# Gated linear attention beside routed experts: differences of the values spread over partitions by a DMA per step instead of by TensorE, and ScalarE as the source of expert weights and biases

## What is computed

```
q = silu(xn Wq) * 16**-0.5;  f = xn Wf;  v = xn Wi;  k = 1 - sigmoid(f)         # 8 heads of 16
S_t = sigmoid(f_t)[:, None] * S_(t-1) + k_t[:, None] * v_t[None, :]             # per head, over 256 tokens
o_t = q_t S_t;   attention = rmsnorm(o) * g_weight @ Wo
# experts: each token goes to 2 of 8, chosen by a hyperbolic distance of project(xn Wp + bp)
# to the centroids, with softmax weights w
experts = sum over the 2 chosen of  w_e * (gelu(xn W1_e + b1_e) W2_e + b2_e)    # 128 -> 512 -> 128
```

## Time and profile before

| | |
|---|---|
| Median of 3 runs | 232.7 us (232.62 to 233.45) |
| Profiled execution, its time | 233.13 us |
| Its span, first to last instruction | 231.4 us |
| Mean granted TensorE clock | 0.911 of full |
| Busy: PE, DVE, POOL, ACT | 191.2, 170.8, 117.6, 104.2 us |
| DMA | 24.45 MB, 106 GB/s |

### The profile page before, as it was taken

How to read it: one execution, slowest core, us unless ns; L and a number is a source line. 1 busy time by engine, 2 the same in 40 slices (tenths; PEclk the granted TensorE clock), 3 DMA queues, 4 the chain that set the end, 5 groups by cost and what they waited for, 6 DMA issues and landing times.

```text
span 231.4 us, 4464 instructions
## 1 busy us (share of the span) xinstructions
PE 191.2 (83%) x1266; PEld 152.0 (66%) x1266; DVE 170.8 (74%) x382; ACT 104.2 (45%) x350; POOL 117.6 (51%) x135
## 2 busy tenths in 40 slices
PE   8692999979589895987999999997789799265890
PEld 7591765456378784867887879886666788123390
DVE  2976930875996986459669979855977687999675
ACT  3439694851364634436434469762554545000011
POOL 7870000002775888776858558787868463302000
PEclk9769799997959998899999999999999999855799
DMA  6681323232753544342334434432444300192015
GB/s 184 178 244 40 97 71 69 46 69 50 221 141 80 130 131 124 82 121 84 118 86 111 122 104 125 146 108 91 125 135 125 81 26 14 29 285 55 0 34 147
DMA packets 21783, 24.45 MB, mean 106 GB/s; under 512 B 2890, under 2 KB 13823, under 8 KB 21760
## 3 DMA queue, kind: packets, MB, share of 16 engines
q1 hardware_dynamic: 17904, 18.91, 29.2%
q0 software_dynamic: 2496, 4.66, 7.6%
q10 hardware_dynamic: 1360, 0.59, 0.9%
HBM read 18.38 MB, written 4.65 MB: 100 GB/s over the span
## 4 chain that ended last, share of the span: by engine, by line
PE 63%; DVE 10%; ACT 10%; issue 8%; another core or an unknown queue 4%; DMA 1%; ACTq 1%; DVEq 0%
PE banks L986 16%; PE banks L976 13%; PE banks L930 6%; PE banks L919 5%; PE banks L837 4%; DVE state L1298 3%; PE banks L968 2%; PE banks L917 2%; ACT xn_t L716 2%; PE banks L835 2%; ACT xn L635 2%; PE banks L954 2%; DVE x_sb L1372 2%; PE banks L792 2%
## 5 line engine op out<-in xcount | busy, mean ns | idle before, releaser
L1298 DVE TENSOR_TENSOR_SCAN state<-gate,banks 128x516 f32<-128x516 f32 x64 | 78.0, 1222 | 21.1 <-PE banks L919 16.4
L475 POOL DMA_INDIRECT xs<-normalised_rows,source x39 | 41.3, 1060 | 49.1 <-DVE source L1283 39.3
L716 ACT ACTIVATE xn_t<-banks,b 128x128 f32<-128x128 f32 x156 | 44.8, 375 | 34.2 <-PE banks L976 25.6
L986 PE MATMUL banks<-w,xn_t 128*128 x312 | 48.6, 287 | 12.2 <-ACT xs_t L709 10.1
L486 POOL DMA_INDIRECT expert_rows_out<-xn_t,place x39 | 42.1, 1081 | 30.5 <-ACT xn_t L725 17.1
L986 PEld LDWEIGHTS banks<-w,xn_t 128*128 128x128 f32 x312 | 41.0, 196 | 20.4 <-issue 20.1
L976 PE MATMUL banks<-xs_t,w 128*128 128x128 f32 x312 | 46.6, 284 | 0.5 <-ACT xs_t L709 0.5
L976 PEld LDWEIGHTS banks<-xs_t,w 128*128 128x128 f32 x312 | 41.5, 199 | 4.0 <-issue 3.4
L919 PE MATMUL banks<-dv,spread 128*128 128x258 f32 x128 | 33.5, 347 | 9.5 <-DVE state L1298 9.5
L1309 DVE TENSOR_TENSOR qstate<-state,q_t 128x512 f32<-128x512 f32 x52 | 36.5, 703 | 0.0
L919 PEld LDWEIGHTS banks<-dv,spread 128*128 128x128 f32 x128 | 20.9, 206 | 14.5 <-DVE state L1298 13.0
(11 more groups left out here) (239 smaller groups left out, 262.1 us busy)
## 6 DMA issues: line engine op xcount, KB each, us to landing
w<-in_L_ffn_W_dram SPq DMA_DIRECT2D x39, 256.0 KB
y_rows<-expert_rows_out SPq DMA_DIRECT2D x8, 256.0 KB, 4.9
x_sb<-_attn_hidden_states_dram SPq DMA_DIRECT2D x4, 256.0 KB, 4.1
normalised_rows<-xn SPq DMA_DIRECT2D x4, 256.0 KB, 2.3
xs<-normalised_rows,source POOLq DMA_INDIRECT x39
expert_rows_out<-xn_t,place POOLq DMA_INDIRECT x39
state<-dv SPq DMA_DIRECT2D x4, 129.0 KB, 2.2
dv<-dv SPq DMA_DIRECT2D x4, 129.0 KB, 2.2
```

The lines of the kernel that those rows point to most:

```text
L475: V.indirect_dma_start(out=xs[t % XRS][:], out_offset=None, in_=xn_dram, in_offset=bass.IndirectOffsetOnAxis(ap=source[:, t:t + 1], axis=0 ...
L716: last = A.activation(hg[t % HGS][:, c * P:(c + 1) * P], bank[6 + t % 2][:, c * P:(c + 1) * P], ACT.Gelu, bias=b1[:, bass.ds(e, 1), c:c + ...
L986: ins = M.matmul(expert_out, hg[t % HGS][:, c * P:(c + 1) * P], w2[:, bass.ds(e, 1), c * D:(c + 1) * D].rearrange("p o f -> p (o f)"), sta ...
L1298: V.tensor_tensor_scan(state[n % STATES][:].rearrange("p b t -> p (b t)"), gate[:, batches_of(g), :].rearrange("p b t -> p (b t)"), pair[n ...
```

## The change

1. **Spread by DMA.** `spread_v`, `less_high_part`, the swaps, `spread`, `minus` and the fp32r tiles are gone. A kind "d" of `project` makes the differences, ACT copies them to `dv_rows[g]` (which are the tiles `state[g]`), SP writes them to DRAM, and for each step SP reads 8 rows of it, each 16 times, into one of `SPREADS = 6` tiles. The scan has both inputs in SBUF. `STATES` is 4, not 6.
2. **Multiplications.** All 64 `times_q` are DVE's.
3. **First weights.** All of W1 (2 MB) is loaded once; ACT copies an expert's part to one of three tiles for each tile of rows.
4. **Biases b2.** All are in SBUF on each partition; ACT writes an expert's row to the PSUM tile in which layer two then accumulates. L917, L1294 and what led to them are gone. `expert_out` is double.
5. **Order of the front.** Centroids and `bp` are turned unnormalised, and what divides by their norm moves behind; ACT squares all 16 routing products (DVE did 6). The counts of the experts stand between `project("d", 2)` and `project("f", 2)`; the values follow the inversion; the "s" projections move into steps 7, 9, 11 and 13. `places()` stands on DVE after the scan of step 2.
6. **Loop and end.** Units are 20 per three steps from step 4 on. Roots of the first three groups are taken together from step 56 on. At the end group 3's expert rows are added around `add_up(3)`, and group 2's last.

```diff
-    STATES = 6
+    STATES = 4
+    SPREADS = 6
-    W1S = 4
+    W1S = 3
-    PER_STEP = 7
-    FIRST_STEP = 2
+    UNITS_OF_STEPS, STEPS_OF_UNITS = 20, 3
+    FIRST_STEP = 4
-    ON_POOL = tuple(n for n in range(5, STEPS) if n % 5 == 0)
+    SUMS_AT = (7, 9, 11, 13)
+    DV_ROW = 576
+    dv_dram = nc.dram_tensor("value_differences", (G, P, DV_ROW), F32).ap()
+        dv = [sb(f"dv{i}", [P, GB, TP]) for i in range(SPREADS)]
+        dv_rows = [state[g][:].rearrange("p b t -> p (b t)") for g in range(G)]
...
# SP
+            def send_differences(g):
+                sp.wait_ge(s_taken, taken("d", g))
+                sp.dma_start(dv_dram[g, :, 0:GB * TP], dv_rows[g]).then_inc(s_dvs[g], 16)
+
+            def load_differences(n):
+                g, j = n // DK, n % DK
+                if n % DK == 0:
+                    sp.wait_ge(s_dvs[g], 16)
+                if n >= SPREADS:
+                    sp.wait_ge(s_scan, n - SPREADS + 1)
+                sp.dma_start(dv[n % SPREADS][:].rearrange("p b t -> p (b t)"),
+                             bass.AP(tensor=dv_dram.tensor, offset=(g * P + first_of(j)) * DV_ROW,
+                                     ap=[[DV_ROW, H], [0, DK], [1, GB * TP]])).then_inc(s_dv[n % SPREADS], 16)
+
+            send_rows(0)
+            send_rows(1)
+            send_differences(0)
+            send_rows(2)
+            send_differences(1)
+            for n in range(SPREADS):
+                load_differences(n)
+            send_rows(3)
+            sp.dma_start(w1[:], w1_in.rearrange("e d f -> d e f")).then_inc(s_w1, 16)
+            sp.dma_start(b2[:], b2_in.unsqueeze(0).to_broadcast([P, E, D])).then_inc(s_b2, 16)
+            send_differences(2)
+            send_differences(3)
+            for n in range(SPREADS, STEPS):
+                load_differences(n)
...
# ACT
+            def first_weights(t, e):
+                if t >= W1S:
+                    act.wait_ge(s_l1, t - W1S + 1)
+                A.copy(w1_of[t % W1S][:], w1[:, bass.ds(e, 1), :].rearrange("p o f -> p (o f)")).then_inc(s_w1of, 1)
+            def bias(t, e):
+                if t >= 2:
+                    act.wait_ge(s_yb, t - 1)
+                A.copy(expert_out[t % 2], b2[:, bass.ds(e, 1), :].rearrange("p o d -> p (o d)")).then_inc(s_b2f, 1)
...
                 if s < TILES:
+                    gelu(s, expert_of(s))
                 if s > 0:
                     expert_rows(s - 1)
+                    if s + 1 < TILES:
+                        bias(s + 1, expert_of(s + 1))
                 if s + 2 < TILES:
                     turned(s + 2)
+                    first_weights(s + 2, expert_of(s + 2))
...
# PE, second layer
+                    pe.wait_ge(s_b2f, t + 1)
+                ins = M.matmul(expert_out[t % 2], hg[t % HGS][:, c * P:(c + 1) * P],
                                w2[:, bass.ds(e, 1), c * D:(c + 1) * D].rearrange("p o f -> p (o f)"),
-                               start=(c == 0), stop=(c == FC - 1))
+                               start=False, stop=(c == FC - 1), skip_group_check=True)
...
# DVE
             def scan(n):
                 g = n // DK
-                dve.wait_ge(s_vb, n + 1)
+                dve.wait_ge(s_dv[n % SPREADS], 16 * (n // SPREADS + 1))
                 dve.wait_ge(s_taken, taken("f", g))
+                if n < G:
+                    dve.wait_ge(s_dvs[n], 16)
...
-                                     pair[n % 2].rearrange("p b t -> p (b t)")[:, BANK - TP:BANK + TP], 0.0,
-                                     ALU.mult, ALU.add).then_inc(s_scan, 1)
+                                     dv[n % SPREADS][:].rearrange("p b t -> p (b t)"), 0.0, ALU.mult, ALU.add).then_inc(s_scan, 1)
...
             scan(0)
             for n in range(STEPS):
                 if n + 1 < STEPS:
                     scan(n + 1)
+                if n == 1:
+                    places()
...
+            g = G - 1
+            dve.wait_ge(s_yg[g], 16 * TOPK)
+            link(add_rows(g, 0))
+            add_up(g)
             dve.wait_ge(s_ot, G)
             V.tensor_tensor(o_sq[:], o_t[:], o_t[:], ALU.mult).then_inc(s_osq, 1)
+            link(add_rows(g, 1))
+            mean(g, added[:, 0:BPG])
```

More of the change, by code:

```diff
@@ L623, in _ @@
             channel_raw(2)
+            for n in range(PER_BANK):
+                squares_of_projection(n)
             channel_raw(3)
[L625 removed]
+            for n in range(PER_BANK, NB):
                 squares_of_projection(n)
[L627 to L631 removed]
             def normalise(g):
@@ L1015, in _ @@
                     pe.wait_ge(s_w2, 16)
-                    pe.wait_ge(s_b2of, BPG)
+                    for rows in expert_out:
+                        last = M.matmul(rows, ident[:], ident[:], start=True, stop=True)
+                    last.then_inc(s_primed, 1)
                     expert_turn(0)
@@ L1327, in finish, with add_attention, roots @@
+            def add_attention(n, rows):
+                return V.scalar_tensor_tensor(out=acc[:, n, :], in0=rows, scalar=rms[:, 1, n:n + 1], in1=x_sb[:, n, :], op0=ALU.mult, op1=ALU.add)
+            def roots(first, last, done):
+                tiles = slice(first * BPG, last * BPG)
+                dve.wait_ge(s_mean, last)
+                for k, ins in enumerate(rsqrt(rms[:, 1, tiles], rms[:, 0, tiles], rms[:, 2, tiles])):
                     ins.then_inc(s_rms, 1)
                     yield
-                    dve.wait_ge(s_rms, done + k + 2)
@@ L1342, in _, with finish_early @@
-            finishing = None
+                    dve.wait_ge(s_rms, done + k + 1)
+            def finish_early():
+                yield from roots(0, EARLY, 0)
+                dve.wait_ge(s_att_sb, EARLY)
+                for g in range(EARLY):
+                    for j in range(BPG):
+                        ins = add_attention(g * BPG + j, att[:, g, j * D:(j + 1) * D])
+                        if j == BPG - 1:
+                            ins.then_inc(s_acc, 1)
+                        yield
@@ L1343, in _, with add_rows @@
+            def add_rows(g, k):
+                for n in range(g * BPG, (g + 1) * BPG):
+                    ins = V.scalar_tensor_tensor(out=acc[:, n, :], in0=y_rows[:, k, n, :], scalar=weight[:, k, n:n + 1],
+                                                 in1=acc[:, n, :], op0=ALU.mult, op1=ALU.add)
+                return ins
+            finishing = finish_early()
             scan(0)
@@ new lines, in _ @@
+                for half in range(2):
+                    if n < DK:
+                        next(of_tokens, None)
+                    elif n >= EARLY * DK + MEAN_AT:
+                        if n == EARLY * DK + MEAN_AT and half == 0:
+                            mean(EARLY - 1, norm2_ps)
+                        else:
+                            for _ in range(FINISH_EACH):
+                                next(finishing, None)
+                    elif n % DK == MEAN_AT and half == 0:
+                        mean(n // DK - 1, norm2_ps)
+                    if half == 0:
+                        times_q(n)
```

622 lines of the change are left out of this document (217 added, 405 removed).

## The result

| | before | after |
|---|---|---|
| Median of 4 runs each | 232.66 us (231.64 to 233.45) | 224.09 us (222.55 to 225.48) |
| Ratio, 95% interval | | 0.963 [0.954, 0.972] |
| Profiled execution, its span | 233.13 us, 231.4 us | 225.48 us, 223.7 us |

Faster, by 3.7%; the prediction was 194 us, 17% faster, with 183 to 213 as its range. The mechanism that it named is there, and 30 us that it counted on are not. Executions of one kernel differ by up to some 5%: a median here is of all of them, a ratio of the faster ones of both kernels.

What follows compares the result with a forecast made beforehand. It saw a ring of PE, DVE and POOL with nearly equal sums as the bound. DVE's 167.6 us, 11.7 for engines holding one another up and 13.3 of end gave a span of 192.6, forecast 194 us, range 183 to 213.

Steps and rivals of the forecast that it cites:

- DVE's own sum: DVE from scan 2 to the last multiplication: 62 x 1.72 us plus 11 us of other work, 117.6 us.
- Front: Ahead of the loop: counts at 31 us, `own` at 40.5, scan 2 waiting for a DMA until 50, first fetch at 52.
- Scan and multiplication: DVE's step in the loop: scan from SBUF kept at 1.22 us, step with multiplication 1.72 us.
- Loads: Differences' loads in the loop: lower half of 0.85 to 2.75 us a step, under DVE's 1.9, hidden by six buffers.
- rival (c): Loads on eight engines at 106 to 157 ns a packet, 2.35 us each, 201 to 205 us; shares chances 0.24 and 0.07.
- the slower rival: DVE waits before the scan for each load, over 2.9 us a load, slower than before; chance 0.07.
- ACT: ACT's work in the loop: 2.54 us a tile, 99 us for 39, some 13 us of other work, 112 us.
- Rival (a): ACT waits 0.5 us per tile, last tile at 182, 205 us in all; shares chance 0.24 for 200 to 213.
- rival (b): POOL's DMAs 0.3 us longer while DVE reads two SBUF inputs, about 208 us; shares chance 0.24 for 200 to 213.
- The step that failed: Loop: DVE, POOL and ACT ending within 6 us hold one another up; a tenth of DVE's 117.6 us, 11.7.
- The sum of POOL: Loop before: POOL's DMAs and multiplications, 129 us from the first fetch at 56.3, over at 185 us.
- End: From the last multiplication to the end: 13.3 us instead of 15.2, as eight of 16 additions move ahead.

Runs made afterwards that it cites:

- e6: Kernel after with only the first 4 of 39 expert tiles, scans, products, gathers and their loads whole (steps alone): 188.4 us, 0.799.
- e13: Whole kernel after with GpSimd's 78 indirect transfers replaced by plain ones of fixed rows, issued by SyncE: 193.55 us, 0.831.
- e2: Kernel after without ScalarE's copy of the first weights; TensorE reads resident weights of expert t mod 8: 222.5 us, 0.949.
- e1: Kernel after with every scan cut to 64 of 516 columns, all else kept: 218.1 us, 0.929.
- e5: Kernel after with the steps' work cut to nearly nothing and six loads of differences, experts whole (experts alone): 213.0 us.
- e14: Whole kernel before with the indirect transfers replaced by plain ones of fixed rows, issued by SyncE: 219.4 us, 0.939.
- e18: Kernel after, steps' work cut to nearly nothing, all transfers indirect, but fetch indices from a fixed table of 128 neighbouring rows: 188.4 us, 0.843.
- e17: Kernel after, steps' work cut to nearly nothing, 39 fetches indirect from GpSimd, 39 returns plain from SyncE: 185.7 us, 0.831.
- e11: Kernel after, steps' work cut to nearly nothing, all 78 indirect transfers replaced by plain ones of fixed rows from SyncE: 182.65 us, 0.778.

## Why the prediction was wrong, step by step

The prediction's span was 192.6 us, the profiled one is 223.7. The 31.1 us between them are four terms. Scan 2 starts at 46.7 us, not 50: -3.3. DVE's own sum is 120.7 us, not 117.6: +3.1. What DVE loses between scan 2 and the last multiplication, 206.98 - 46.70 - 120.7 = 39.6 us, not 11.7: +27.9. The end is 16.7 us, not 13.3: +3.4.

**Front.** Right. The counts were said for 31 us and came at 28.5, `own` for 40.5 and came at 38.0, scan 2 for 50 with a DMA as its releaser and came at 46.7 with that one. The first fetch starts at 49.6, not 52; before it was 56.3.

**Scan and multiplication.** Right. 1.24 us a scan out of SBUF against 1.22 assumed, and two undisturbed scans start 1.72 us apart (60.73 and 62.45 us). The lower bound that the prediction gave for the scan is a slip: with 298 ns that don't grow, 516 columns come to 0.81 us, not 0.93. Nothing hangs on it. DVE's other work in the loop was put too low: 120.7 us for the whole, by e6, where 117.6 were taken.

**Loads.** Right that they hide; rival (c) and the slower rival did not come. The only wait of the 64 scans is the front's 5.5 us, and in e13, where the steps run at DVE's pace, four scans wait 1.4 us in all for their loads. In 110 to 130 us, after:

```profile
q1 hardware_dynamic: 1088, 2.11, 31.4%
...
dv<-value_differences SPq DMA_DIRECT2D x8, 258.0 KB
```

That is 0.314 x 16 x 20 / 1,088 = 92 ns a packet, below the 106 taken; the share is 0.31, not 0.5, since the steps come slower. (The 157 ns of the earlier trace rows were too high beside these: 80 packets stand there, not 64, which makes 125.) The packets also tell how many engines carry a load. The trace has 1,024 of 2,064 bytes and 64 of 4 bytes: 128 rows and eight short packets a load, where the earlier trace rows has 64 rows and 16 short ones. And q1 has 9 or more packets under way at once for only 1.5 of the 20 us, where in the window of the earlier trace rows it has 16 or 17 for 3.1 of 5 us. So it is eight engines, as the Trainium skill, "DMA: Bandwidth & Descriptors" ("Why a DMA increments its semaphore by 16 and not by 1"), has it by its rule; the trace agrees. The condition of rival (c) was there, its price was not: 16 rows of 98 ns make 1.6 us, with POOL's 0.25 still under the 1.9 of a step.

**ACT.** Its sum is right: the copy of the first weights 620 ns against 650, the biases 269 against 270. Rival (a) asked for 0.5 us of wait a tile. The waits before the gelu are 10.1 us in all, 0.26 a tile, but taking the copy away (e2) gives nothing to be measured.

**POOL, rival (b).** The mechanism is right, and the reason against it was wrong. Between 91.5 and 100 us, with DVE at full pace, a DMA takes 1.38 to 1.47 us; from 122.00, while DVE stands:

```profile
118.55 1.38 POOL L439 DMA_INDIRECT xs<-normalised_rows,source  x1 [0.30 <-issue]
120.23 1.46 POOL L450 DMA_INDIRECT expert_rows_out<-xn_t,place  x1 [0.30 <-issue]
122.00 0.98 POOL L439 DMA_INDIRECT xs<-normalised_rows,source  x1 [0.31 <-remote]
123.28 1.02 POOL L450 DMA_INDIRECT expert_rows_out<-xn_t,place  x1 [0.30 <-issue]
124.60 0.97 POOL L439 DMA_INDIRECT xs<-normalised_rows,source  x1 [0.31 <-issue]
```

I had read the earlier trace rows as DMAs beside DVE's multiplications. They were two neighbouring ones of the short kind, and the mean of the earlier trace rows hid the others. The mean rose by 0.22 us, 17 us in all, where (b) said 0.3. The GPSIMD Engine Reference of the Trainium skill ("Key points") names this contention, and the trace agrees, 0.97 to 1.02 against 1.38 to 1.47 us. But e1 takes nearly all of it away, and only some 6 to 8 us go with it. It isn't what decides the time.

**The step that failed** is "Three in-order engines within 6 us of each other hold one another up. Before, that cost 200 - 185 = 14 to 15 us in 144, a tenth". The sum of POOL explained the stretch before all but a tenth, and I took that for its cause and the rest for friction that scales. Both were wrong. The term for it, 11.7 us of loss, measured 39.6. The experts' tiles had a pace of their own, 3.4 us (e5), which no engine's sum shows, since it lies in waits. The kernel before ran its tiles at that pace already (3.35 us; 2.93 with plain transfers, e14), and the steps' work lay under it for the most part. Take much of the steps' work away, and the pace stays: the first fetch came 6.8 us earlier and the loads of the experts' rows only 1.3 us (199.39 us against 200.67 in the earlier trace rows). (The 224 us of the kernel after are 11 more than the experts take alone; what makes these wasn't told apart.) With plain transfers the loss is 174.09 - 46.24 - 120.7 = 7.2 us, below the 11.7 taken, and the kernel takes 193.55 us, where 194 was forecast; the half us is luck, since the smaller loss (-4.5), the earlier front (-3.8), DVE's sum (+3.1) and the longer end (+4.0) cancel. Before with plain transfers takes 219.4. The change is then worth 26 us, not 8.6. The other 13 of the forecast 39 us are the share of the late reports in the kernel before, which the change does not take away.

**End.** 16.7 us, not 13.3. The eight additions of group 3 moved as said (those left at the very end are group 2's, 2.31 us for eight at 216.89, against 4.54 for 16). I had not counted that PE's granted clock would be lower there, 0.70 of full in the window of the end where before it was 0.95: the output product takes 2.08 us and the norms 1.71, where they took 1.16 and 0.95, and DVE waits 1.97 for the norms, where it waited 1.31. The kernel ends with PE's and ACT's additions of group 1 (220.33 us), no more with DVE's.

**What is shown and what is not.** Shown: with indirect transfers the experts alone take 213 us, 207 without registers, and with plain fetches 183, whatever the returns are; the waits without a releaser go with them, and so they do in both whole kernels. Not shown: how an indirect fetch delays a report of PE. Nor is it shown that the indirection does it: a plain fetch also reads 128 neighbouring rows in place of those that the routing chose, and e18, meant to part the two, falls in the set where the kernel before was fast. For the same reason e17 leaves open whether fetches alone suffice, and why that set had no late reports stays open. In the whole kernel the 30 us also hold POOL's own 17 us of lengthened DMAs; the two were not told apart there, only with the experts alone, where the DMAs were at their shortest.

## What to carry to other kernels

Before you sum engines, look for a pace that none of them shows: run each stream alone, with the other's work cut to nothing. Two such runs gave 213 and 188 us here, and the kernel took 224. A wait "remote" beside a releaser that by its record is long done isn't friction; find what it goes away with. And order transfers by who waits, down to the last one: two of 258 KB ahead of 4 MB gave 5.9 us at the front, and a load left behind 2.5 of these took 4.3 back.

## What was not expected of the hardware

- TensorE's results were seen by ScalarE and VectorE 2.5 to 5.5 us late, several at one moment, some six times in the loop after; 39.9 us of such waits after, 16.4 before, none in the six kernels with plain transfers for some or all of them (e11, e13 to e17), and none either in e18, whose transfers are all indirect.
- A load of eight DRAM rows that are read 16 times each ran on eight of the 16 DMA engines, at 98 ns a row of 2,064 bytes.
- An indirect DMA's time on GpSimd, 0.97 to 1.02 us alone, is 1.38 to 1.47 beside VectorE at full pace.
- The kernel before took 230 to 241 us in four sets of the study and 221 to 226 in the fifth, for a reason that no run showed.
